# Recurrence sums on accumulating DMAs instead of GpSimd, a ring of three steps, the first two steps summed on VectorE, and two steps moved behind the start of attention

## The reference

```
ek = exp(min(k, 30));  ekv = ek * v;  decay = exp(-exp(w)) * (0.5 + 0.5 tf)      # v = k
nf, df = forward scans  a = a*decay + ekv,  b = b*decay + ek   over the 256 tokens
nb, db = the same scans backwards
num = nf + nb - ekv + exp(min(u + k, 30)) * v
den = df + db - ek  + exp(min(u + k, 30))
gate(r) = sigmoid(r) * num / max(den, 1e-8) * (0.8 + 0.2 tf)
x = x + attention0(gate0(x));  x = x + ffn0(gate1(x))       # softmax over rows + softmax over columns; fp8 matmul
x = x + attention1(gate2(x));  x = x + ffn1(gate3(x))       # rope, block-causal softmax; ternary weights, squared relu
```

## Time and profile before

| | us |
|---|---|
| median of 3 runs (lowest, highest) | 493.34 (492.98, 493.89) |
| the profiled execution, its own time | 492.78 |
| its span in the trace | 490.9 |
| start, to the first vector instruction of slot 0 | 63.24 |
| slots 0 to 30, to the end of the last scan | 175.86 |
| tail of attention 0 and feed-forward 0, about | 34.9 |
| layer 1 | 216.9 |

### The profile page before, as it was taken

One profiled execution on the slowest core, in us unless ns is written; L12 is line 12 of the kernel. 1 busy time (PEld: TensorE's weight loads), 2 busy tenths in 40 slices (PEclk: granted clock), 3 DMA queues, 4 the chain that ended last, 5 costly groups with the idle time before them and its releaser, 6 DMA issues.

```text
span 490.9 us, 4921 instructions
## 1 busy us (share of the span) xinstructions
PE 268.1 (55%) x1763; PEld 160.3 (33%) x1766; DVE 336.9 (69%) x533; ACT 184.0 (37%) x272; POOL 136.0 (28%) x123
## 2 busy tenths in 40 slices
PE   0020144224445445434563657879888989965754
PEld 0020032112223222212232334456465666524522
DVE  1998999799879897998637666443446533087453
ACT  6531144523563226334231132254074543234322
POOL 2445434556256635654620112010200000000000
PEclk9996566557656765756655669596699585596877
DMA  7000000000000200000300000000000000000010
GB/s 240 6 0 1 0 0 1 1 0 1 1 0 1 87 0 1 0 0 1 160 13 0 0 1 0 0 1 1 1 1 1 1 1 1 0 1 1 32 33 21
DMA packets 4055, 7.52 MB, mean 15 GB/s; under 512 B 1088, under 2 KB 2496, under 8 KB 3648
## 3 DMA queue, kind: packets, MB, share of 16 engines
q1 hardware_dynamic: 4032, 7.21, 4.2%
HBM read 6.16 MB, written 1.05 MB: 15 GB/s over the span
## 4 chain that ended last, share of the span: by engine, by line
DVE 39%; PE 31%; issue 10%; ACT 8%; POOL 8%; DMA 1%; SPq 1%; ACTq 0%; DVEq 0%; POOLq 0%
PE PS L1109 7%; DVE db L628 7%; PE PM L1057 5%; DVE df L628 4%; DVE nb L628 3%; DVE nf L628 3%; PE PM L954 3%; PE PO L1127 3%; DVE rsum L696 3%; POOL df L281 3%; PE PM L1006 3%; POOL df L282 3%; DVE EU L864 2%; ACT E L468 2%; PE PO L1191 2%
## 5 line engine op out<-in xcount | busy, mean ns | idle before, releaser
L798 DVE TENSOR_REDUCE kp<-PS 128x2 f32<-128x256 f32 x64 | 32.2, 553 | 33.9 <-PE PS L1088 33.9
L981 PE MATMUL PO<-E,vt 128*32 128x256 f32 x256 | 31.0, 633 | 40.2 <-DVE ytok L723 25.3
L386 ACT ACTIVATE df<-df,lnmin 128x512 f32<-128x512 f32 x16 | 11.5, 720 | 101.3 <-POOL df L282 101.3
L989 PE MATMUL PO<-ident,yc 128*128 128x128 f32 x64 | 18.7, 387 | 55.6 <-ACT yc L453 55.6
L468 ACT ACTIVATE E<-PS,negc,escale 128x1024 f32<-128x1024 f32 x32 | 38.3, 1198 | 22.6 <-PE PS L968 22.6
L539 ACT ACTIVATE E<-PS 128x384 f32<-128x384 f32 x64 | 28.0, 492 | 38.9 <-PE PS L1109 38.8
L281 POOL TENSOR_TENSOR df<-df,db 128x512 f32<-128x512 f32 x16 | 24.9, 1556 | 51.7 <-DVE nb L628 51.6
L696 DVE TENSOR_REDUCE rsum<-E 128x4 f32<-128x1024 f32 x32 | 38.1, 1208 | 1.4 <-ACT E L468 1.4
L279 POOL TENSOR_TENSOR mv<-EU,vf 128x512 f32<-128x512 f32 x12 | 25.0, 2081 | 42.7 <-DVE EU L618 42.7
L628 DVE TENSOR_TENSOR_SCAN db<-DT,ek 128x512 f32<-128x512 f32 x16 | 34.5, 2158 | 0.0
L954 PE MATMUL PM<-ident,kp 128*128 128x128 f32 x128 | 23.9, 348 | 15.7 <-DVE kp L651 11.3
(11 more groups left out here) (159 smaller groups left out, 652.3 us busy)
## 6 DMA issues: line engine op xcount, KB each, us to landing
kT<-in_kT SPq DMA_DIRECT2D x4, 256.0 KB, 4.9
xT<-in_xT SPq DMA_DIRECT2D x4, 256.0 KB, 6.0
G<-in_attn SPq DMA_DIRECT2D x1, 1024.0 KB, 6.8
ek<-in_w SPq DMA_DIRECT2D x1, 1024.0 KB, 4.9
ekv<-in_w SPq DMA_DIRECT2D x1, 1024.0 KB, 7.0
out<-G SPq DMA_DIRECT2D x8, 128.0 KB, 1.7
w<-in_attn SPq DMA_DIRECT2D x1, 512.0 KB, 7.3
cond<-in_cond SPq DMA_DIRECT2D x1, 128.0 KB, 4.9
```

Of the source, the lines that this page charges most:

```text
L798: nc.vector.tensor_reduce(kp[:, b % 2, u * H + 2 * j:u * H + 2 * j + 2, D], PS[:, at0:at0 + 2, lo:hi], AX, ALU.max, negate=True).then_inc( ...
L981: ins = nc.tensor.matmul(PO[SLOT * g:SLOT * (g + 1), q % 2, 0:T], vt[:, b % 2, v * H + 4 * c + g, :], E[:, (2 * q + g // 2) % 4, g % 2, v ...
L989: ins = nc.tensor.transpose(PO[:, q % 2, T + u * P:T + (u + 1) * P], yc[:, q % 2, u * P:(u + 1) * P], ident[:])
```

## The change

Four things change together.

1. **Who sums.** From step 2 on, POOL computes nothing for a step. It issues two DMAs that add in SBUF: `fwd += mid` (both halves, m and mv, 128 x 1024 f32, 512 KB) once the two forward scans are done, then, when that has landed, `fwd += bwd` (again 512 KB) once the backward scans are done. mv moves to DVE (L601 after). For steps 0 and 1 DVE adds both sums itself, the denominator first.
2. **Where the steps stand.** Only steps 0 and 1 remain in the start; steps 2 to 15 go to slots 0, 2, 4, 6, 9, 11, 13, 16, 18, 20, 22, 25, 27, 29 (`WKV0`). The Ln and Exp stand three slots behind the scans, the gate four.
3. **Buffers.** The ring has three steps instead of two. exp(u + k) and the decay tile are made per step by `prepare(n)` on ACT, one slot ahead of the scans, and the decay tile holds one step.
4. **Aliases of layer 1.** Tiles of the later stages that lay in the old buffers lie elsewhere; no instruction of those stages changes.

```
-        EU = [sb(f"EU{i}", [P, N]) for i in range(2)]
-        DT = [sb(f"DT{i}", [P, N + 8]) for i in range(2)]
-        RING = 2
+        RING = 3
+        DT = [sb(f"DT{i}", [P, SEG + 8]) for i in range(2)]
+        mid = sb("mid", [P, RING, 2, SEG])
+        fwd = sb("fwd", [P, RING, 2, SEG])
+        bwd = sb("bwd", [P, RING, 2, SEG])
...
+        EARLY = 2
+        WKV0 = {(16 * i) // 7: EARLY + i for i in range(LAYERS * B - EARLY)}
...
+        def steps0(p, lag):
+            return [n for at, n in WKV0.items() if at + lag == p]
```

POOL's part of a step:

```
             def wkv(n):
                 l, b, r = wkv_at(n)
-                m = EU[l % 2][:, seg(b)]
-                pool.wait_ge(S["m_done"], n + 1)
...
-                pool.wait_ge(S["scan_done"], 4 * (n + 1))
-                link(nc.gpsimd.tensor_tensor(df[:, r], df[:, r], db[:, r], ALU.add))
-                nc.gpsimd.tensor_tensor(df[:, r], df[:, r], m, ALU.add).then_inc(S["den_ready"], 1)
-                if n >= B:
-                    link(nc.gpsimd.tensor_tensor(nf[:, r], nf[:, r], nb[:, r], ALU.add))
-                    nc.gpsimd.tensor_tensor(nf[:, r], nf[:, r], mv[:, r], ALU.add).then_inc(S["num_ready"], 1)
+                pool.wait_ge(S["mv_done"], n + 1)
+                pool.wait_ge(S["scan_done"], 4 * n + 2)
+                nc.gpsimd.dma_start(fwd[:, r], mid[:, r], accum_op=ALU.add).then_inc(S[f"mid_added{r}"], 16)
+                pool.wait_ge(S[f"mid_added{r}"], added(n))
+                pool.wait_ge(S["scan_done"], 4 * n + 4)
+                nc.gpsimd.dma_start(fwd[:, r], bwd[:, r], accum_op=ALU.add).then_inc(S[f"back_added{r}"], 16)
```

ACT's preparation, its Ln, and its loop over the slots:

```
+            def prepare(n):
...
+                for h in range(HALF):
+                    nc.scalar.activation(mid[:, r, 0, h * T:(h + 1) * T], kT[:, seg(b, h * T, T)], ACT.Exp,
+                                         bias=vec[:, 1, l, h:h + 1]).then_inc(S["prep_done"], 1)
...
+                if n >= 2:
+                    act.wait_ge(S["scan_done"], 4 * (n - 1))
+                nc.scalar.activation(DT[n % 2][:, 0:SEG].rearrange("p (h t) -> p h t", t=T)[:, :, 1:T],
...
             def wkv(n):
-                act.wait_ge(S["den_ready"], n + 1)
...
+                if n < EARLY:
+                    act.wait_ge(S["den_early"], n + 1)
+                else:
+                    act.wait_ge(S[f"back_added{r}"], added(n))
+                nc.scalar.activation(fwd[:, r, 0], fwd[:, r, 0], ACT.Ln, bias=lnmin[:]).then_inc(S["ln_done"], 1)
...
             for p in range(SLOTS0):
                 b, j = divmod(p, PAIRS)
-                if 2 <= p < B * PAIRS + 2 and wkv_slot(p - 2) >= 0:
-                    wkv(wkv_step(p - 2))
+                for n in steps0(p, 3):
+                    wkv(n)
+                for n in steps0(p, -1):
+                    prepare(n)
```

DVE's product, its start, and the end of its slot loop:

```
+                nc.vector.tensor_tensor(mid[:, r, 1], mid[:, r, 0], vf[:, seg(b)], ALU.mult).then_inc(S["mv_done"], 1)
...
+            inputs(0)
+            ahead(0, 0)
+            behind(0, 0)
+            summed(0, 0, "den_early")
+            ahead(0, 1)
+            behind(0, 1)
+            summed(0, 1, "num_early")
+            gate(0)
+            gated(0, 0)
...
+            inputs(1)
+            ahead(1, 0)
+            behind(1, 0)
             normed(0)
-            wkv(3)
+            summed(1, 0, "den_early")
+            ahead(1, 1)
+            behind(1, 1)
             low_parts(0)
+            summed(1, 1, "num_early")
+            gate(1)
...
-                if p < B * PAIRS and wkv_slot(p) >= 0:
-                    wkv(wkv_step(p))
+                for n in steps0(p, 4):
+                    gate(n)
+                for n in steps0(p, 0):
+                    wkv(n)
```

More of the change, by code:

```diff
@@ L186, in seg, with steps1, added @@
             return slice(b * SEG + lo, b * SEG + lo + n)
-        def halves(tile):
-            return tile[:, 0:N].rearrange("p (b h t) -> p b h t", b=B, h=HALF)
         def wkv_at(n):
             return n // B, n % B, n % RING
-        def wkv_slot(p):
-            return {0: 0, 3: 1, 6: 2}.get(p % PAIRS, -1)
-        def wkv_step(p):
-            return B + 3 * (p // PAIRS) + wkv_slot(p)
+        EARLY = 2
+        WKV0 = {(16 * i) // 7: EARLY + i for i in range(LAYERS * B - EARLY)}
+        WKV1 = {}
+        def steps0(p, lag):
+            return [n for at, n in WKV0.items() if at + lag == p]
+        def steps1(p, lag):
+            return [n for at, n in WKV1.items() if at + lag == p]
+        def added(n):
+            return 16 * len([m for m in range(EARLY, n + 1) if m % RING == n % RING])
         def vt_col(buf, row):
@@ L297, in _ @@
             nc.gpsimd.memset(epsc[:], EPS_RMS).then_inc(S["pads_set"], 1)
+            for i in range(2):
+                nc.gpsimd.memset(DT[i][:, 0:SEG + 1:T], 0.0).then_inc(S["decay_edge"], 1)
             pool.wait_ge(S["cond_tanh"], 1)
@@ L342, in _ @@
                 b, j = p // PAIRS + 2, p % PAIRS
+                for n in steps1(p, 0):
+                    wkv(n)
                 if j == 1 and b < B:
@@ L631, in wkv, with ahead, behind @@
-                if n >= 1:
-                    gate(n - 1)
+            def ahead(n, i):
+                l, b, r = wkv_at(n)
+                src = (ek, ekv)[i]
+                nc.vector.tensor_tensor_scan(fwd[:, r, i], DT[n % 2][:, 0:SEG], src[:, seg(b)], 0.0, ALU.mult,
+                                             ALU.add).then_inc(S["scan_done"], 1)
+            def behind(n, i):
+                l, b, r = wkv_at(n)
+                src = (ek, ekv)[i]
+                nc.vector.tensor_tensor_scan(bwd[:, r, i][:, ::-1], DT[n % 2][:, 1:SEG + 1][:, ::-1],
+                                             src[:, seg(b)][:, ::-1], 0.0, ALU.mult,
+                                             ALU.add).then_inc(S["scan_done"], 1)
@@ new lines, in summed, with wkv @@
+            def summed(n, i, done):
+                r = n % RING
+                dve.wait_ge(S["scan_done"], 4 * n + 2 + 2 * i)
+                link(nc.vector.tensor_tensor(fwd[:, r, i], fwd[:, r, i], bwd[:, r, i], ALU.add))
+                dve.wait_ge(S["mv_done"], n + 1)
+                nc.vector.tensor_tensor(fwd[:, r, i], fwd[:, r, i], mid[:, r, i], ALU.add).then_inc(S[done], 1)
+            def wkv(n):
+                inputs(n)
+                for i in range(2):
+                    ahead(n, i)
+                for i in range(2):
+                    behind(n, i)
```

137 lines of the change are left out of this document (43 added, 94 removed).

## The result

The kernel after takes 466.52 us (median of 4 runs, 461.79 to 467.70) against 493.16 for the kernel before (4 runs), ratio 0.9465, 95% interval 0.937 to 0.956. The prediction was 460 in a range of 448 to 486. The profiled execution took 467.70 with a span of 465.9.

A forecast was written before the change was run, and what follows sets the result against it. VectorE's own order, with its waits, was taken to bound start and slots. Start 38.0, slots 160.9 and waits 8.1 put the last scan at 207.0; the tail's 12.0 gave 219.0 against 251.6, a span of 458.3, so 460 us, range 448 to 486.

The forecast's parts named there:

- The start, 25.2 us: Stretch before slot 0: with only steps 0 and 1 there, slot 0 begins on VectorE at 38.0 instead of 63.24 us.
- The scans' collisions, 11.2 us: Slots: 11 scans, each slowed by 1.02 us by POOL's products, lose that delay; 11.2 us saved.
- v over sums, 10.8: Slots: 16 products v over sums fall from 966 to 290 ns without POOL's arithmetic beside them; 10.8 us saved.
- L = 5.4: Assumed time from issue to landing of one accumulating 512 KB DMA: 4.9 us for two reads plus half a microsecond for issue.
- The low parts' waits, 7.4 us: Slots 6 and 22: `low_parts` waits for the sums, 2L - 7.3 and 2L - 6.9, together 7.4 us at L = 5.4.
- sum of 160.9: Slots to the last scan's end, without waits for the new DMAs: 175.9 less 39.2 saved plus 24.2 added us.
- The tail, 2L + 1.2 = 12.0 us: Last scan to last `group_out`: step 15 has no slot cover, so copies wait behind its Ln; 12.0 us, 9.1 without the DMA.
- The quick sum: Rival: sums land in L of 3.1 to 4.2, the waits vanish and the kernel takes 449 us; chance 0.12.
- Collisions stay: Rival: descriptor making on POOL holds VectorE as arithmetic does, 28 DMAs at 1.0 us, 488 us; chance 0.06.
- The price of a slow adder: Rival: L of 6.3 to 9 adds waits at `low_parts`, tail and `sums`; 469 us at 6.5, 476 at 8, 486 at 9; chance 0.19.
- 2L + 0.4 + 8.5: Slots, when every pair of steps waits: us from one scan's end to that of the step four slots on, 6.5 rounds.
- slower than before: Rival: ScalarE's blocked queue makes the kernel not faster from L = 9.5, about 500 us at L = 10; chance 0.12.

The follow-up runs named there:

- run 5: Kernel after, with each of the two accumulating DMAs of steps 2 to 15 replaced by one GpSimd addition at the same place: 487.49 us, ratio 0.9915 to the kernel before.
- run 9: Kernel after, with four accumulating DMAs of 256 KB per step, the denominator's first, and the logarithm waiting for the denominator's two only: 458.00 us, ratio 0.9349.
- run 2: Kernel after, with the two 1 MB weight loads waiting for the last accumulating DMA instead of starting after the last scan: 458.64 us, ratio 0.9331.
- run 3: Kernel after, with step 15's Ln, Exp and gate moved from slots 32 and 33 to slot 39, behind attention's last copies: 453.83 us, ratio 0.9254.
- run 6: Kernel after, with the four small `v_rows` products on VectorE in slot 5 of each eight instead of on GpSimd: 465.33 us, ratio 0.9484.
- run 8: Kernel after, with four steps ahead of the first scores, later ones in slots 0, 3, 6 of each eight, and step 15's Ln, Exp and gate in slot 39: 447.93 us.
- run 7: Kernel after, with a third accumulating 512 KB DMA of zeros per step, between the two and waited for: 503.09 us, ratio 1.0276.
- run 10: Kernel after, with logarithm and exponential two slots behind the scans instead of three and the gate three instead of four, DMAs kept: 504.25 us, ratio 1.0279.
- run 4: Kernel after, with all four steps of gate 0 ahead of the first scores and steps 4 to 15 in slots 0, 3, 6 of each eight: 456.55 us, ratio 0.9297.

## Why the prediction was right or wrong

**The sum.** Luck has a part in how near 460 lies to 466.5. The slots came out 4.5 us shorter than forecast and the tail 6.8 longer, and the two nearly cancel; most of the rest is the 4.8 us of layer 1.

**The bound.** Right. VectorE is busy in 157.9 of the 164.5 us of the slots, and its order is the clock.

**The start, 25.2 us.** Right: slot 0 on VectorE at 38.48 (predicted 38.0), the first projection at 19.20 (19.3).

**The scans' collisions, 11.2 us, and v over sums, 10.8.** Right in kind, shown by run 5: with POOL adding, the slots are 28.9 us longer. Mis-sized by what the sum left out: `v_rows` stayed on POOL and costs 4.5 us in m and v over sums; the term for v over sums took all sixteen to 290 ns, and they measure 420.

**L = 5.4.** The DMA lands after 4.5 us, and the next issue comes 4.8 us after it, here in the kernel after's slots:

```profile
57.60 0.85 POOL L273 DMA_DIRECT2D fwd<-mid  x1 [6.82 <-DVE fwd L609]
...
62.42 0.87 POOL L276 DMA_DIRECT2D fwd<-bwd  x1 [3.97 <-DMA fwd<-mid]
```

So L was 0.6 to 0.9 too long: the 4.9 us for two reads was about the whole price, and the half microsecond for the issue lies inside it. By the Trainium skill, page "DMA: Bandwidth & Descriptors", section "Anatomy of one DMA — SWDGE (gpsimd) path", the estimates are 4.4 us for 512 KB and 3.2 for 256 KB if each byte is counted twice, 3.2 and 2.6 if once; the rows of 4.5 and 3.3 (run 9) agree with counting twice.

**The low parts' waits, 7.4 us.** They were 1.7 (0.44 and 1.26 in slots 6 and 22; none in slot 14). With L = 4.85 the same terms give 5.2. The 3.5 us between have no experiment of their own. With 1.7 for these waits and 4.5 for the collisions left in, the sum of 160.9 would be 167.1; the slots took 164.5. So 2.6 us, spread over fourteen steps, stay unexplained.

**The tail, 2L + 1.2 = 12.0 us.** Wrong, 18.8. The step failed at "step 15 has no slot cover": it named the DMA's wait, and not what else the last scan releases. Two 1 MB loads start then and double the landing, which makes the logarithm 4.7 us late (run 2). And from the logarithm's start the forecast had 3.4 us to the last `group_out`, which leaves no room for the product between the two copies (1.93 by its own rows): it is 4.7 us in run 2, and 6.1 in the kernel after, whose TensorE has idled longer and runs that product and its turns at the lower clock. With the loads away the tail is 12.8 (run 2), near the forecast only because L was taken too long: with L = 4.85 the term gives 10.9. With the logarithm behind the copies the tail is 10.05 (run 3).

**The stretch behind it, left alone.** 4.8 us longer, the other of the two lengths. It isn't the change's: four of the ten runs of the kernel after are of the short kind, and runs 2, 3, 5, 6 and 8 carry most of the change and show the short one. What selects the one or the other is open. The prediction named a layer 1 longer by more than 2 us as a sign of being wrong; with two lengths 5 us apart that sign tells nothing.

**The rivals.** The quick sum (L to 4.2) did not come, though L lay near it. "Collisions stay" fell: scans beside POOL's DMA issues take 1.20 us and an issue 0.87. By the Trainium skill, page "SBUF — State Buffer", section "Who interferes with whom", a VectorE instruction with two SBUF inputs contends with a GpSimd instruction that reads SBUF, and for `tensor_tensor` it is inferred that it does not shut descriptor making out. The trace agrees with the first (2.04 against 0.68 us) and, for the scans and the gate, with the second (0.87 us per issue).

**The price of a slow adder was far too low.** The prediction had 469 at L = 6.5, 476 at 8, and no gain only from 9.5. Runs 7 and 10 make the sums late for ScalarE by two unlike edits, by 7 us and by one slot (about 5), and cost 38 to 40 us each. Three landings (3 x 4.85 us) are two of 7.3, for which the forecast gives about 473; the 14.9 us that run 7 has between last scan and logarithm are 2L - 2.2 at L = 8.5, for which it gives about 481. Run 7 took 503. The failed step is the round of "2L + 0.4 + 8.5", 25.9 us for two steps at L = 8.5: it took 29.1 us in run 7 and 30.0 in run 10. One part of that is a wait that the forecast did not look for, that of the norm on ScalarE's copy: 15.7 of the 42.8 us of VectorE's waits in run 10, but only 3.7 of 39.1 in run 7, where the row sums and the low parts, which it did look at, make 33.3. Why those cost so much more than the round had isn't traced further. A straight line from 464 us at L = 4.85 to run 7 crosses the 490 us of the kernel before at an L of about 6.5 to 7.3, an estimate; so the chance for "slower than before", 0.12 from L = 9.5, should have begun there. The forecast stood because L came out at 4.85, on the flat side of an edge that lay closer than it said.

**Part 2, never priced alone.** The prediction's terms held it: two more steps in the slots cost 11.6 + 3.4 + 0.6 = 15.6 us. It did not set this against what the two cost in the start, 13.5 by run 4. Attention starting sooner was worth nothing, as the same engine paces both stretches, and with four steps first the kernel is even faster (7.4 us in run 4; 4.6 in run 8 against run 3).

## What to carry to other kernels

When sums go from an engine to DMAs, the queue behind the instruction that waits for them decides: place the waiting instruction by the slowest landing, and list every instruction that stands behind it and who needs each; five microseconds of lateness cost nothing or forty here. Ask of the last one what else its releaser sets off, since a big load begun at the same moment can double its landing. And moving work across a border that one engine paces on both sides gains nothing by itself: price such a move alone.
